# An attention and FFN sandwich on one core: probabilities and normalised x transposed through VectorE and DRAM in place of TensorE

## The chip, the cores and the metric

The kernel runs on one core of a Trainium2 chip. The metric is the device time of one execution in microseconds; the median of three runs of the kernel before is 426.01 us (425.57 to 428.9).

## The reference

For eight batches of 1024 rows of 256 numbers in float32:

```
x = x + layernorm(attn(layernorm(x)))        # one head, causal, Wq Wk Wv Wo of 256 x 256
x = x + layernorm(layernorm(x) @ W[idx] + b[idx])
attn(x): q = x@Wq; k = x@Wk; v = x@Wv
         softmax(mask(q k^T) / 16) v @ Wo
idx    = argmax(log_softmax(logits) - log(-log(u)))     # one of eight FFN weights
```

## The kernel before

A batch is cut into NT = 8 tiles of 128 rows, in NP = 4 pairs. Wq and Wk are folded into one matrix a, Wv and Wo into wvo, before the first batch. TensorE multiplies in a reduced float32 form; to keep precision each operand is kept as two halves: `hi` is rounded by ScalarE, `lo` is the value less `hi`, by VectorE. `product` (L805) makes three passes per block: lo x hi, hi x lo, hi x hi.

The steps of a batch, each named by a letter and a number in the order lists:

- S n: scores of row tile n against the n + 1 tiles up to it (two PSUM score buffers). M n (VectorE, L707): masks them, writes neg_scores, gives the row's maximum. E n (ScalarE, L549): exponentials to `probs`, with their sum.
- T n: TensorE transposes the n + 1 blocks of `probs` into one or two PSUM banks (L908); ScalarE rounds them to pT_hi (L441), VectorE subtracts to pT_lo (L613).
- V n: values of two tiles, with wvo. O n: probabilities times values, 3 (n + 1) products.
- O on ScalarE: sum of squares of the O row, and o_ez from the exponentials' sum; C n: variance on VectorE (o_ve, L735) and its power -1/2 on GpSimd (o_rstd, L387); R n (L741, VectorE): y = O x o_rstd + x, which frees the bank.
- N, K, Y, F, U, Z per pair: statistics of y (L749 to L756 on VectorE, power and shift on GpSimd), K: yn by ScalarE (L583), Y: its transposes (L932) and halves, F: product with the FFN weights, bias added by VectorE (L762), squares by ScalarE (L591), U: f_ve and f_rstd, Z (L778): out = f x f_rstd + y, then the store.
- L, H, X, G prepare the next batch: L statistics of x (L627 to L634 on VectorE, power and shift on GpSimd), H xn on ScalarE (L464), X transposes of xn per pair (L819) and halves, G n: a quarter of g = a^T xT, six products of 512 columns, and halves.

Each engine runs its own written list of steps (PE_ORDER, ACT_ORDER, DVE_ORDER, POOL_ORDER, and _LAST for batch 7). Batches 0 and 7 are straight-line code, batches 1 to 6 a hardware loop (Fori). All PSUM outputs except the scores rotate over four banks in the order of TensorE's list: a job waits until VectorE has drained the bank's previous one. The sync engine's queue issues four loads of x for the batch after next, each behind R of its pair, and then four stores.

Of the kernel before, what the change touches and what calls it, by code (L numbers as in the profile page):

```python
# [5 lines left out]
def sandwich_block_kernel(  # L6
# [28 lines left out]
    f32 = mybir.dt.float32  # L35
# [18 lines left out]
    PAR = NT * D  # L54

# [10 lines left out]
    PE_ORDER = """S0 V0 S1 V1 T0 S2 T1 S3 O0 V2 T2 O1 S4 T3 V3 O2 S5 O3 T4 S6 T5 S7 X0 Y0 O4 T6 O5 T7 O6 X1 Y1  # L66
        O7 F0 G0 Y2 X2 F1 X3 F2 Y3 G1 G2 F3 G3"""
    ACT_ORDER = """V0 E0 E1 V1 T0 E2 O0 T1 V2 T2 O1 E3 H0 T3 V3 E4 O2 O3 E5 T4 K0 T5 E6 K1 X0 Y0 O4 T6 E7 O5 T7
        H1 H2 O6 Y1 H3 X1 O7 K2 G0 Y2 F0 X2 K3 X3 F1 Y3 F2 G1 G2 F3 G3"""
    DVE_ORDER = """M0 M1 L0 V0 M2 T0 V1 L1 T1 C0 M3 R0 V2 L2 T2 M4 C1 V3 T3 R1 N0 M5 C2 C3 R2 R3 N1 M6 T4 T5 M7  # L70
        X0 Y0 C4 R4 T6 C5 L3 R5 T7 C6 N2 R6 X1 Y1 C7 F0 R7 N3 G0 Y2 F1 U0 X2 Z0 X3 F2 U1 Y3 U2 Z1 G1
        F3 Z2 U3 G2 G3 Z3"""
    POOL_ORDER = """C0 L0 L1 C1 C2 C3 N0 N1 C4 L2 C5 L3 C6 N2 C7 N3 U0 U1 U2 U3"""


    PE_LAST = """V0 S0 V1 S1 T0 S2 V2 T1 S3 O0 T2 O1 S4 T3 S5 O2 T4 O3 S6 V3 T5 O4 S7 Y0 T6 O5 T7 O6 Y1 F0 O7
        Y2 F1 F2 Y3 D11 Y4 F3 D12 F4"""
    ACT_LAST = """E0 V0 V1 T0 E1 V2 T1 E2 O0 E3 T2 O1 T3 E4 T4 O2 O3 E5 K0 E6 V3 T5 O4 Y0 T6 E7 O5 K1 T7 O6 Y1
        K2 F0 O7 Y2 K3 Y3 F1 K4 Y4 F2 F3 F4"""
    DVE_LAST = """M0 V0 M1 M2 V1 T0 V2 T1 C0 M3 M4 C1 R0 T2 R1 T3 N0 M5 C2 R2 C3 T4 M6 R3 V3 N1 C4 T5 R4 M7 Y0  # L80
        T6 C5 R5 T7 N2 C6 F0 R6 Y1 U0 N3 C7 Y2 F1 R7 N4 F2 Y3 U1 Z0 Z1 Y4 U2 F3 U3 F4 Z2 U4 Z3 Z4"""
    POOL_LAST = """C0 C1 C2 N0 C3 N1 C4 C5 N2 C6 U0 N3 C7 N4 U1 U2 U3 U4"""

    PE_BEFORE = "D22 W0 W1 D13 X0 A0 X1 D25 W2 G0 D6 X2 X3 G1 A1 G2 G3"
    ACT_BEFORE = "W0 H0 J0 H1 X0 A0 X1 B0 H2 H3 G0 J1 X2 X3 G1 U0 A1 U1 G2 U2 G3 E0"
    DVE_BEFORE = "L0 L1 W1 B0 J0 L2 L3 X0 A0 X1 W2 B1 G0 X2 X3 U0 G1 A1 U1 G2 G3"
# [3 lines left out]

    def tiles_of(unit, last):
# [17 lines left out]
    def jobs_of(steps):  # L112
        for kind, n in steps:
            if kind == "T":
                for g in range(len(t_groups(n))):
                    yield (kind, n, g)
            elif kind in "VOYFXGA":
                yield (kind, n, 0)

    SPLIT = "ATVYXG"
    def is_split(job):
        return job[0] in SPLIT

    def places(jobs, act_jobs, job0, split0):
        splits = {j: split0 + 1 + at for at, j in enumerate(filter(is_split, act_jobs))}
        return {j: (job0 + at, splits.get(j, 0)) for at, j in enumerate(jobs)}

    before = places(jobs_of(steps_of(PE_BEFORE)), jobs_of(steps_of(ACT_BEFORE)), 0, 0)  # L130
    JOB0, SPLIT0 = len(before), sum(map(is_split, before))
    full, final = (places(jobs_of(steps_of(pe)), jobs_of(steps_of(act)), JOB0, SPLIT0)
                   for pe, act in ((PE_ORDER, ACT_ORDER), (PE_LAST, ACT_LAST)))
    PER, SPER = len(full), sum(map(is_split, full))
    assert PER % NB == 0

    class Job:

        def __init__(self, b, last, kind, n, g=0, before=0):

            place, splits = (final if last else full)[(kind, n, g)]
            self.bank = place % NB
            self.offset = place // NB - before * (PER // NB)
            self.used = self.offset + b * (PER // NB)
            self.splits = splits + b * SPER

    class Before:
        def __init__(self, kind, n):  # L150
            place, self.splits = before[(kind, n, 0)]
            self.bank, self.offset = place % NB, place // NB
            self.used = self.offset

    def g_job(b, n):

        return Before("G", n) if isinstance(b, int) and b == 0 else Job(b, False, "G", n, before=1)

    x_rows = x.rearrange("b (t p) d -> b p t d", p=PART)
    out_rows = out.rearrange("b (t p) d -> b p t d", p=PART)  # L160

    ctx = ExitStack()
    with ctx:
# [41 lines left out]
        o_ez = sb("o_ez", [PART, NT])  # L205
        o_ve = sb("o_ve", [PART, NT])
# [26 lines left out]
        wf_raw = sb("wf_raw", [PART, KC, D])  # L233
# [4 lines left out]
        ident = sb("ident", [PART, PART])  # L238
        mask = sb("mask", [PART, S])
# [19 lines left out]
        hi_ready = sem("hi_ready")  # L259
        scores_ready = sem("scores_ready")  # L260
# [26 lines left out]
        halves_ready = sem("halves_ready")  # L287
        memsets = sem("memsets")
# [8 lines left out]
        wf_centred = sem("wf_centred")  # L297
        wf_hi_ready = sem("wf_hi_ready")
# [10 lines left out]

        def x_tile(b, t, n=1):  # L310

            return x_sb[:, bass.ds((b % 2) * PAR + t * D, n * D)]

        @block.sync
        def _(sp):
            def load_x(b, p, parity_at):
                sp.dma_start(x_sb[:, bass.ds(parity_at + 2 * p * D, 2 * D)],
                             x_rows[b, :, 2 * p:2 * p + 2, :]).then_inc(x_loaded[p], 16)

            def store(b, unit, last=False):  # L320
# [15 lines left out]
            load_x(0, 2, 0)  # L336
            load_x(0, 3, 0)
# [35 lines left out]
        def _(pool):  # L373
# [5 lines left out]
                                    pattern=[[-1, PART]], channel_multiplier=1).then_inc(consts_ready, 1)  # L379
            nc.gpsimd.memset(mask[:, :], 0.0).then_inc(memsets, 1)  # L380
# [38 lines left out]
            for p in range(NP):  # L419
                x_scales(0, p)  # L420
# [563 lines left out]
```

## Time and profile before

| | |
|---|---|
| median of three runs | 426.01 us |
| span of the profiled execution, from first to last instruction | 424.3 us (the page gives no other time of that execution) |
| busy: TensorE, VectorE, ScalarE, GpSimd | 98%, 80%, 71%, 28% |
| TensorE's own work on the chain that ended last | 93% |
| moved by DMA | 18.46 MB, 44 GB/s over the span |

Busy is the share of the span in which an engine executes something. Durations of single instructions overlap their successors on all engines, so what one costs in a row of many is read from the distance of starts. The chain that ended last is followed back from the last instruction and says which engine the time passed through.

### The profile page before, as it was taken

The page shows a single profiled execution, that of the slowest core. Times are in us where ns is not written, and L with a number is a line of the kernel's source. Part 1 is how long each engine was busy: PE and PEld are TensorE (multiplying, and loading weights), DVE is VectorE, ACT ScalarE, POOL GpSimd, SP SyncE. Part 2 cuts the span into 40 slices and gives each one's busy share as a digit, 9 for nine tenths or more (in the row PEclk, how much of TensorE's full clock was granted, in tenths as well). Part 3 has the DMA queues.
Part 4 walks back from the last instruction along what each step waited for, and adds up shares of the span by engine and source line. Part 5 has one row for each costly group of instructions (what it writes and reads, how often), then busy time and mean ns, then how long its engine had stood idle before and what let it go on. Part 6 is the DMA issues. An engine that isn't in the chain of part 4 may idle for free.

```text
span 424.3 us, 9812 instructions
## 1 busy us (share of the span) xinstructions
PE 414.0 (98%) x3045; PEld 393.2 (93%) x3045; DVE 339.8 (80%) x1010; ACT 299.1 (71%) x854; POOL 118.3 (28%) x237
## 2 busy tenths in 40 slices
PE   7999999999999999999999999999999999999993
PEld 7789999999999999999999999999999999999993
DVE  4578778987898878887788878898788887876776
ACT  5886877668766687568866687666885678756563
POOL 3103333232322232123421323223232224302133
PEclk9999999999999999999999999999999999999998
DMA  6310012110120101201021001201012000020003
GB/s 198 90 49 26 26 25 76 52 39 14 51 81 18 49 25 42 82 9 40 25 66 57 25 25 48 76 25 49 13 37 99 0 0 0 25 75 2 2 0 101
DMA packets 18951, 18.46 MB, mean 44 GB/s; under 512 B 1140, under 2 KB 18932, under 8 KB 18932
## 3 DMA queue, kind: packets, MB, share of 16 engines
q1 hardware_dynamic: 18660, 17.96, 13.5%
q10 hardware_dynamic: 272, 0.26, 0.2%
q8 instruction: 10, 0.16, 0.2%
q14 instruction: 9, 0.07, 0.1%
HBM read 9.83 MB, written 8.39 MB: 43 GB/s over the span
## 4 chain that ended last, share of the span: by engine, by line
PE 93%; DMA 2%; ACT 2%; DVE 1%; issue 0%; POOL 0%; SPq 0%; POOLq 0%; DVEq 0%
PE bank L805 54%; PE score L805 23%; PE bank L908 7%; PE bank L932 3%; PE bank L819 3%; DMA wq<-in_L_attn_Wq_dram 1%; DMA bias_raw<-in_L_ffn_b_dram 1%; PE score L891 1%; PE score L847 0%; PE bank L865 0%; POOL f_rstd L387 0%; PE score L835 0%; DVE out_sb L778 0%; ACT squares_junk L591 0%; ACT sums_junk L470 0%
## 5 line engine op out<-in xcount | busy, mean ns | idle before, releaser
L387 POOL TENSOR_TENSOR o_rstd<-o_ve,minus_half 128x1 f32<-128x1 f32 x64 | 35.2, 550 | 193.8 <-DVE o_ve L735 193.8
L805 PE MATMUL bank<-v_hi,pT_lo 128*128 128x256 f32 x288 | 84.6, 294 | 0.0
L805 PE MATMUL bank<-v_hi,pT_hi 128*128 128x256 f32 x288 | 81.4, 283 | 0.0
L805 PE MATMUL bank<-v_lo,pT_hi 128*128 128x256 f32 x288 | 81.3, 282 | 0.0
L805 PE MATMUL score<-xT_hi,g_lo 128*128 128x384 f32 (+4 forms) x176 | 63.7, 362 | 0.0
L805 PE MATMUL score<-xT_hi,g_hi 128*128 128x384 f32 (+4 forms) x176 | 61.1, 347 | 0.0
L805 PE MATMUL score<-xT_lo,g_hi 128*128 128x384 f32 (+4 forms) x176 | 61.1, 347 | 0.0
L549 ACT ACTIVATE probs<-neg_scores,neg_max 128x128 f32<-128x128 f32 (+3 forms) x64 | 49.7, 776 | 14.0 <-DVE neg_max L707 13.5
L805 PEld LDWEIGHTS bank<-v_lo,pT_hi 128*128 128x128 f32 x288 | 55.0, 191 | 0.4
L805 PEld LDWEIGHTS bank<-v_hi,pT_lo 128*128 128x128 f32 x288 | 54.9, 191 | 0.3
L805 PEld LDWEIGHTS bank<-v_hi,pT_hi 128*128 128x128 f32 x288 | 54.9, 191 | 0.0
L707 DVE CUSTOM_DVE_ANT_0 neg_scores<-score,mask 128x128 f32<-128x128 f32 (+3 forms) x64 | 48.2, 755 | 7.6 <-PE score L805 7.5
L574 ACT ACTIVATE squares_junk<-bank 128x256 bf16<-128x256 f32 x64 | 24.5, 383 | 40.3 <-PE bank L805 39.8
L613 DVE TENSOR_TENSOR pT_lo<-bank,pT_hi 128x384 fp32r<-128x384 f32 (+2 forms) x96 | 49.6, 551 | 0.8
L441 ACT ACTIVATE pT_hi<-bank 128x384 fp32r<-128x384 f32 (+2 forms) x96 | 43.1, 484 | 2.2 <-PE bank L908 2.0
L908 PE MATMUL bank<-ident,probs 128*128 128x128 f32 x288 | 42.0, 273 | 0.0
L741 DVE SCALAR_TENSOR_TENSOR y<-bank,o_rstd,x_sb 128x256 f32<-128x256 f32 x64 | 30.8, 481 | 11.1 <-POOL o_rstd L387 11.0
L591 ACT ACTIVATE squares_junk<-f_sb 128x256 bf16<-128x256 f32 x64 | 26.3, 419 | 16.7 <-DVE f_sb L762 16.7
L583 ACT ACTIVATE yn<-y,y_shift,y_rstd 128x256 f32<-128x256 f32 x64 | 35.0, 597 | 4.3 <-POOL y_shift L393 4.3
L387 POOL TENSOR_TENSOR f_rstd<-f_ve,minus_half 128x2 f32<-128x2 f32 (+1 forms) x33 | 24.1, 731 | 49.6 <-DVE f_ve L769 49.6
L805 PE MATMUL bank<-wf_hi,yT_lo 128*128 128x256 f32 x128 | 37.3, 292 | 0.4 <-DVE yT_lo L613 0.4
L805 PE MATMUL bank<-wvo_hi,xT_lo 128*128 128x256 f32 x128 | 36.9, 288 | 0.0
(112 smaller groups left out, 1130.5 us busy)
## 6 DMA issues: line engine op xcount, KB each, us to landing
x_sb<-in_L_attn_x_dram SPq DMA_DIRECT2D x32, 256.0 KB, 2.7
out_dram<-out_sb SPq DMA_DIRECT2D x31, 256.0 KB, 2.1
wq<-in_L_attn_Wq_dram ACTq DMA_DIRECT2D x1, 256.0 KB, 4.1
wk<-in_L_attn_Wk_dram SPq DMA_DIRECT2D x1, 256.0 KB, 4.4
wv<-in_L_attn_Wv_dram SPq DMA_DIRECT2D x1, 256.0 KB, 4.2
wo_raw<-in_L_attn_Wo_dram SPq DMA_DIRECT2D x1, 256.0 KB, 4.5
wf_raw<-in_L_ffn_W_dram SPq DMA_DIRECT2D x1, 256.0 KB, 2.7
out_dram<-out_sb SPq DMA_DIRECT2D x2, 128.0 KB, 2.1
```

What stands on the lines that cost most here:

```text
L387: return nc.gpsimd.tensor_tensor(dst[:, n0:n1], ve[:, n0:n1], minus_half[:, n0:n1], ALU.pow)
L441: nc.scalar.activation(dst, src, ACT.Identity).then_inc(hi_ready, 1)
L549: nc.scalar.activation(probs[:, n % 2, here], neg_scores[:, n % 2, here], ACT.Exp, scale=-1.0, bias=neg_max[:, n:n + 1], accum_out=exp_sum ...
L574: nc.scalar.activation(squares_junk[:, 0, n, :], cols(job.bank, D), ACT.Square, accum_out=o_ss[:, n:n + 1])
L583: last = nc.scalar.activation(yn[:, p, t % 2, :], y[:, t, :], ACT.Identity, bias=y_shift[:, t:t + 1], scale=y_rstd[:, t:t + 1])
L591: last = nc.scalar.activation(squares_junk[:, 1, t, :], f_sb[:, p, t % 2, :], ACT.Square, accum_out=f_ss[:, t:t + 1])
L613: nc.vector.tensor_tensor(dst, src, hi.bitcast(f32), ALU.subtract).then_inc(bank_drained[job.bank], 1)
L707: nc.vector.tensor_tensor_reduce(out=masked.rearrange("p (h w) -> p h w", h=h), in0=score[:, n % 2, 0:h, 0:w], in1=mask[:, here].rearrange ...
L741: nc.vector.scalar_tensor_tensor(out=y[:, n, :], in0=cols(job.bank, D), scalar=o_rstd[:, n:n + 1], in1=x_tile(b, n), op0=ALU.mult, op1=ALU ...
L805: last = nc.tensor.matmul(dst, l, r, start=(i == 0), stop=(i == len(passes) - 1))
L819: last = nc.tensor.transpose(cols(job.bank)[:, (2 * k + t) * PART:(2 * k + t + 1) * PART], xn[:, 2 * p + t, k * PART:(k + 1) * PART], iden ...
L908: last = nc.tensor.transpose(cols(job.bank)[:, (t - t0) * PART:(t - t0 + 1) * PART], probs[:, n % 2, t * PART:(t + 1) * PART], ident[:, :])
```

## The change

Probabilities (all of batches 0 to 6, tiles 0 to 3 of batch 7) and xn of batches 1 to 7 are no longer transposed by TensorE. VectorE transposes them in blocks of 32 x 32 (steps Q n and B p) into `p_turn` and `x_turn`; the sync queue writes each pair's buffer to DRAM (P p, and W for the whole of xn) and fetches it back in four DMAs, one for each 32 partitions, with the blocks exchanged between partitions (Q p, R 0). ScalarE rounds the `hi` halves from SBUF (P n, X n), GpSimd subtracts all `lo` halves of the probabilities and those of the second half of xT (X2, X3), VectorE those of the first half (X0, X1).

Other parts:

- y is transposed itself, without yn; F is scaled by y_rstd afterwards (two VectorE operations of 256 columns in place of one of 512). For this the FFN weights' column means are taken off at the start, by two products with a constant matrix.
- The exponentials' sum comes from O: v has two more columns (a constant and zero), so the O products have 258 columns; the squares of O and F take in a constant column, and o_ez, o_ve, f_ve, y_nm, y_ve, x_nm, x_ve leave ScalarE and VectorE. GpSimd adds eps and negates the mean itself.
- All batches are straight-line code; each list has steps of the batch before (marked '), and the sync queue has a list of its own. The new TensorE list puts all scores first. pT has three buffers in place of two; Z writes into f_sb and the store leaves from there.

```diff
-    PE_ORDER = """S0 V0 S1 V1 T0 S2 T1 S3 O0 V2 T2 O1 S4 T3 V3 O2 S5 O3 T4 S6 T5 S7 X0 Y0 O4 T6 O5 T7 O6 X1 Y1
-        O7 F0 G0 Y2 X2 F1 X3 F2 Y3 G1 G2 F3 G3"""
+    PE_ORDER = """S0 O6' Y2' S1 O7' S2 S3 V0 S4 S5 Y3' V1 S6 V2 S7 O0 O1 F1' V3 O2 F2' Y0 O3 F3' O4 O5 F0 G0 G1 Y1 G2 G3"""
+    ACT_ORDER = """G3' E0 O6' Y2' E1 H0 O7' H1 E2 H2 E3 V0 E4 P0 P1 Y3' E5 V1 H3 V2 E6 P2 O0 P3 O1 E7 F1' V3 O2 P4 P5 Y0 O3
+        F2' F3' O4 X0 X1 X2 O5 X3 F0 G0 P6 G1 P7 Y1 G2"""
+    DVE_ORDER = """Y1' G2' M0 G3' Q0 L0 L1 K0 M1 R6' Y2' Q1 K1 L2 B0 K2 M2 R7' B1 M3 Q2 N3' Q3 M4 V0 B2 M5 L3 Q4 Q5 K3 Y3'
+        V1 M6 B3 V2 Q6 M7 R0 F1' Q7 R1 V3 Z1' N0 R2 F2' Y0 F3' R3 N1 Z2' X0 X1 R4 F0 R5 Z3' N2 G0 Z0 G1"""
+    POOL_ORDER = """N2' C6' L0 L1 C7' L2 N3' P0 P1 L3 P2 C0 P3 C1 U1' C2 P4 P5 C3 U2' N0 C4 U3' N1 C5 X2 X3 U0 P6 P7"""
+    SP_ORDER = """P0 A3' Q0 P1 Q1 P2 W0 Q2 P3 R0 A0 Z1' Q3 A1 Z2' A2 Z3' Z0"""
+    PE_LAST = """V0 O6' S0 O7' S1 S2 S3 Y2' S4 S5 Y3' V1 V2 V3 O0 O1 S6 F1' Y0 O2 S7 O3 T4 T5 F2' F3' Y1 O4 T6 O5 F0 T7
+        O6 F1 Y2 O7 Y3 F2 F3 Y4 F4"""
...
+            def fetch(raw, kept, loaded):
+                for q, source in enumerate(kept):
+                    sp.dma_start(raw[q * QUAD:(q + 1) * QUAD].rearrange("a (i r) -> a i r", i=QUADS), source
+                                 ).then_inc(loaded, 16)
...
+                    elif kind == "W":
+                        sp.wait_ge(x_turned, b.count(NP, 0))
+                        sp.dma_start(x_kept.rearrange("p q r -> p (q r)"), x_turn[:, :]).then_inc(x_written, 16)
+                    elif kind == "R":
+                        sp.wait_ge(x_written, b.count(16, 0))
+                        fetch(x_turn[:, :], x_kept.rearrange("(i a) q r -> q a i r", i=QUADS), x_raw_loaded)
+                    elif kind == "P":
+                        sp.wait_ge(p_turned, b.count(NT, 2 * n + 2))
+                        sp.dma_start(p_kept[n].rearrange("p q r -> p (q r)"), p_slot(n)).then_inc(p_written[n], 16)
+                    elif kind == "Q":
+                        sp.wait_ge(p_written[n], b.count(16, 16))
+                        fetch(p_slot(n), p_kept[n].rearrange("(i a) q r -> q a i r", i=QUADS), p_loaded[n])
...  # GpSimd
+                    elif kind == "P":
+                        pool.wait_ge(p_hi_ready, b.count(NT, n + 1))
+                        nc.gpsimd.tensor_tensor(p_half(pT_lo, n), p_quads(n), p_half(pT_hi, n).bitcast(f32),
+                                                ALU.subtract).then_inc(p_lo_ready, 1)
...  # VectorE
+                    elif kind == "Q":
+                        dve.wait_ge(probs_ready, b.count(NT, n + 1))
...
+                        nc.vector.transpose(p_quads(n), probs[:, n % 2, 0:(n + 1) * PART].rearrange(
+                            "p (u q a) -> p u q a", q=QUADS, a=QUAD)).then_inc(p_turned, 1)
```

## Rows read from the trace of the kernel before

**Rows 1.** The page: span, busy times, TensorE in forty slices, chain by engine.

```profile
span 424.3 us, 9812 instructions
PE 414.0 (98%) x3045; PEld 393.2 (93%) x3045; DVE 339.8 (80%) x1010; ACT 299.1 (71%) x854; POOL 118.3 (28%) x237
...
PE   7999999999999999999999999999999999999993
...
PE 93%; DMA 2%; ACT 2%; DVE 1%; issue 0%; POOL 0%; SPq 0%; POOLq 0%; DVEq 0%
```

**Rows 2.** First products of a batch: all, then three starts in time order.

```profile
L891 PE MATMUL score<-xT_first,g_first x32: 271/275/377, 23.3 to 374.7; 128*128 128x128 f32 x32
...
223.20 0.61 PE L891 MATMUL score<-xT_first,g_first 128*128 128x128 f32 x4
273.11 0.61 PE L891 MATMUL score<-xT_first,g_first 128*128 128x128 f32 x4
...
374.36 0.61 PE L891 MATMUL score<-xT_first,g_first 128*128 128x128 f32 x4
```

**Rows 3.** TensorE in time order (start, us), and O6 in the chain.

```profile
203.03 1.06 PE L908 MATMUL bank<-ident,probs 128*128 128x128 f32 x8
203.84 0.36 PE L805 MATMUL bank<-v_hi,pT_lo 128*128 128x256 f32 x1
...
206.44 0.60 PE L819 MATMUL bank<-ident,xn 128*128 128x128 f32 x4
206.88 0.60 PE L932 MATMUL bank<-ident,yn 128*128 128x128 f32 x4
...
204.09 2.52 PE bank L805 x21
```

**Rows 4.** VectorE in time order: a stretch without waits, and two scale-and-adds.

```profile
229.15 0.29 DVE L613 TENSOR_TENSOR pT_lo<-bank,pT_hi 128x128 fp32r<-128x128 f32 x1
229.35 0.68 DVE L613 TENSOR_TENSOR v_lo<-bank,v_hi 128x512 fp32r<-128x512 f32 x1
229.95 0.74 DVE L627 BATCH_NORM_STATS2 x_stats<-x_sb 128x6 f32 x2
230.77 0.25 DVE L630 BATCH_NORM_AGGREGATE x_mv<-x_stats 128x2 f32<-128x6 f32 x2
231.05 0.17 DVE L633 TENSOR_SCALAR x_nm<-x_mv 128x2 f32<-128x2 f32 x1
...
224.97 0.87 DVE L778 SCALAR_TENSOR_TENSOR out_sb<-f_sb,f_rstd,y 128x256 f32<-128x256 f32 x2
225.76 0.28 DVE L707 CUSTOM_DVE_ANT_0 neg_scores<-score,mask 128x128 f32<-128x128 f32 x1
```

**Rows 5.** GpSimd in time order, then the exponentials (ns: shortest, median, longest).

```profile
1.61 0.95 POOL L380 MEMSET mask<- 128x1024 f32 x1
...
232.01 0.55 POOL L387 TENSOR_TENSOR o_rstd<-o_ve,minus_half 128x1 f32<-128x1 f32 x1 [7.41 <-DVE o_ve L735]
232.53 0.70 POOL L387 TENSOR_TENSOR x_rstd<-x_ve,minus_half 128x2 f32<-128x2 f32 x1
...
L549 ACT ACTIVATE probs<-neg_scores,neg_max x64: 390/775/1162, 27.0 to 400.9; 128x128 f32<-128x128 f32 x8, 128x256 f32<-128x256 f32 x8, 128x384 f32<-128x384 f32 x8, 128x512 f32<-128x512 f32 x8
```

**Rows 6.** Stretches (last: clock, DMA share, GB/s); an issue; KB and us to landing.

```profile
4.00:6.00 2.00, 1.35 (x8) 1.05 (x6) 1.24 (x6) 0.00 (x0) 0.01 (x1) 1.00 1.09 371
20.00:25.00 5.00, 4.36 (x26) 3.52 (x25) 1.75 (x4) 4.41 (x13) 0.00 (x0) 1.00 0.54 187
...
0.75 0.45 SPq L317 DMA_DIRECT2D x_sb<-in_L_attn_x_dram  x1
...
x_sb<-in_L_attn_x_dram SPq DMA_DIRECT2D x32, 256.0 KB, 2.7
out_dram<-out_sb SPq DMA_DIRECT2D x31, 256.0 KB, 2.1
```

More of the change, by code:

```diff
@@ L110, in pieces, with __init__, count, other @@
         return (1, w) if w <= BANK else (2, w // 2)
-    def jobs_of(steps):
-        for kind, n in steps:
+    class Batch:
+        def __init__(self, s, ahead):
+            self.known = s + ahead
+            self.first, self.last = self.known == 0, self.known == B - 1
+        def count(self, per, extra):
+            return self.known * per + extra
+        def other(self, by):
+            return Batch(self.known, by)
+        def exists(self, first=0):
+            return first <= self.known < B
@@ L114, in jobs_of @@
+    def jobs_of(turns):
+        for kind, n, ahead in turns:
             if kind == "T":
                 for g in range(len(t_groups(n))):
[L116 to L134, printed above, removed]
+                    yield (kind, n, g, ahead)
+            elif kind in "VOYFG":
+                yield (kind, n, 0, ahead)
+    PE_TURNS, PE_LAST_TURNS = turns_of(PE_ORDER), turns_of(PE_LAST)
@@ L149, in sandwich_block_kernel @@
     class Before:
         def __init__(self, kind, n):
[L151 to L157, printed above, removed]
+            place = BEFORE_JOBS.index((kind, n))
+            self.bank, self.used = place % NB, place // NB
+            self.offset = self.used
+            self.splits = BEFORE_SPLITS.index((kind, n)) + 1
@@ L159, in sandwich_block_kernel, with places_of, follows @@
+    def places_of(order, last):
+        at = {}
+        for s in range(B):
+            for kind, n, ahead in turns_of(order if s < B - 1 else last):
+                at[(kind, n, s + ahead)] = len(at)
+        return at
+    in_dve, in_act = places_of(DVE_ORDER, DVE_LAST), places_of(ACT_ORDER, ACT_LAST)
+    def follows(places, then, first):
+        return first in places and places[first] < places[then]
     x_rows = x.rearrange("b (t p) d -> b p t d", p=PART)
     out_rows = out.rearrange("b (t p) d -> b p t d", p=PART)
+    x_kept = nc.dram_tensor("x_kept", (PART, QUADS, RUN), f32, kind="Internal").ap()
@@ L162, in sandwich_block_kernel @@
+    p_kept = [nc.dram_tensor(f"p_kept{p}", (PART, QUADS, (4 * p + 3) * QUAD), f32, kind="Internal").ap()
+              for p in range(NP)]
     ctx = ExitStack()
@@ L308, in cols, with raw_block, split_block, p_slot @@
             return bank[bk][:, 0:n]
+        def raw_block(c, k):
+            cols_of = x_turn[:, :].rearrange("p (i k t s) -> p k t i s", i=QUADS, k=KC, t=NT)
+            return cols_of[:, k, c * (NT // 2):(c + 1) * (NT // 2), :, :]
+        def split_block(half, c, k):
+            return half[:, k, c * BANK:(c + 1) * BANK].rearrange("p (t i s) -> p t i s", t=NT // 2, i=QUADS)
+        def p_slot(p):
+            at = sum(4 * q + 3 for q in range(p)) * PART
+            return p_turn[:, at:at + (4 * p + 3) * PART]
@@ L369, in _ @@
+            sequence(0, SP_ORDER)
+            for s in range(1, B - 2):
+                sequence(s, SP_ORDER)
+            sequence(B - 2, SP_ORDER)
+            sequence(B - 1, SP_LAST)
             for p in range(NP):
@@ L404, in sequence @@
+            def sequence(s, text):
+                for kind, n, ahead in turns_of(text):
+                    b = Batch(s, ahead)
+                    if not b.exists(kind in "LX"):
+                        continue
+                    t0, t1, p = tiles_of(n, b.last)
                     if kind == "L":
-                        x_scales(b + 1, n)
+                        x_scales(b, n)
                     elif kind == "C":
-                        pool.wait_ge(o_ve_ready, b * NT + n + 1)
-                        rstd(o_rstd, o_ve, n, n + 1).then_inc(o_rstd_ready, 1)
+                        pool.wait_ge(o_squares, b.count(NT, n + 1))
+                        rstd(o_rstd, o_ss, n, n + 1).then_inc(o_rstd_ready, 1)
@@ L426, in _ @@
+            for p in range(NP):
+                x_scales(Batch(0, 0), p)
+            sequence(0, POOL_ORDER)
+            for s in range(1, B - 1):
+                sequence(s, POOL_ORDER)
+            sequence(B - 1, POOL_LAST)
         @block.scalar
@@ L593, in sequence @@
                         last.then_inc(f_squares, 1)
[L595 to L598 removed]
+            sequence(0, ACT_ORDER)
+            for s in range(1, B - 1):
+                sequence(s, ACT_ORDER)
+            sequence(B - 1, ACT_LAST)
         @block.vector
@@ new lines, in sequence @@
+                        for t in range(t0, t1):
+                            last = nc.vector.scalar_tensor_tensor(out=f_sb[:, p, t % 2, 0:D],
+                                                                  in0=bank[job.bank][:, (t - t0) * D:(t - t0 + 1) * D],
+                                                                  scalar=y_rstd[:, t:t + 1], in1=bias[:, :],
+                                                                  op0=ALU.mult, op1=ALU.add)
+                        last.then_inc(bank_drained[job.bank], 1)
```

630 lines of the change are left out of this document (376 added, 254 removed).

## The prediction

> **What bounds the kernel now.** I read the page first: busy shares, the forty slices and the chain of waits [rows 1]. TensorE is busy 98% of a span of 424.3 us, in every slice but the ends, and 93% of the chain that ended last is its own work. VectorE is at 80%, ScalarE at 71%, GpSimd at 28%. The first products of a batch (S0) then give the period [rows 2]: 273.11 - 223.20 = 49.91 us. The first S0 is at 23.3, the last at 374.36, so the span is 23.3 of preparation, 351.1 for seven batches, and 49.9 for the last. TensorE waits for practically nothing inside a period, so taking work off it pays one for one until another engine or a transfer sets the pace.
>
> **What leaves TensorE.** From the start of a group to the next start, eight transposes of probabilities take 203.84 - 203.03 = 0.81, and the product behind them starts its successor 0.08 later than usual, so 0.89 or 0.11 each; a group of four of xn takes 206.88 - 206.44 = 0.44, 0.11 each [rows 3]. A batch has 36 of probabilities and 16 of xn for the next batch: 52 x 0.11 = 5.7 us. The products are untouched: O6's 21 take 2.52, 0.12 each [rows 3], and two more columns on 256 for the 108 O products add 108 x 0.12 x 2/256 = 0.1. TensorE's own need per batch is then 49.9 - 5.7 + 0.1 = 44.3 us. In the last batch only 10 of the 36 leave (1.1 us). The work that the new order carries into the next batch (O6', O7', Y2', Y3', F1' to F3') is 45 + 36 products and 8 transposes, 81 x 0.12 + 0.9 = 10.6 us: it leaves batch 0 and arrives in the last.
>
> **VectorE.** Its real price is the distance of starts, not the duration [rows 4]: 128 columns take 229.35 - 229.15 = 0.20, 512 take 229.95 - 229.35 = 0.60, so a width w costs 0.07 + 1.04 ns x w; two scale-and-adds take 225.76 - 224.97 = 0.79, 0.40 each; two bn_stats with their drain 0.82, two bn_aggr 0.28, and the two small operations behind them end 0.15 later. Per batch of now: M 5.4, pT_lo 5.6, four groups of four 512-wide low halves 9.6, statistics 8 x 1.26 = 10.1, R, Z 3.2 each, F 2.4, o_ve and f_ve 1.3: 40.8, which is the 80%. Removed: pT_lo 5.6, half of xT_lo 1.2, x_nm, x_ve, y_nm, y_ve, o_ve, f_ve 8 x 0.15 + 1.3 = 2.5. Added: F as eight scale-and-adds +0.8, and the 32x32 block transposes, which no row shows. They write as many columns as M reads: 8 x 0.07 + 4608 x 1.04 ns = 5.4 for the probabilities (Q) and 8 x (0.07 + 0.27) = 2.7 for xn (B). That takes one column per 1.04 ns, the nearest row of the same engine and type; at half that rate they would be 7 us dearer, at twice it 3.5 cheaper. Sum: 40.8 - 9.3 + 0.8 + 8.1 = 40.4 us of 44.3, 91%. So VectorE may idle 3.9 us per batch where it now idles 9. I went through the order by hand with these prices: before S7 it has 21.2 us of work in 22.8 of TensorE's, and every M is done before the S two further on asks for it.
>
> **ScalarE** loses yn (64 x 0.6 now), o_ez and the accumulator reads of the exponentials, and P replaces the rounding of pT_hi at equal width. It is lighter and not on the path, except E7, 1.16 us [rows 5], which stands behind P3 and O1.
>
> **GpSimd** gets P (4608 columns) and half of X (1024). It has shown only a memset, 0.95 us for 1024 columns, and powers of one and two columns, 0.55 and 0.70 [rows 5]. The memset's 0.93 ns a column is the low end. [...] What is queued behind P matters more: C3 (o_rstd) stands behind P4 and P5, but O3's bank is wanted only four jobs later, 5.4 us on.
>
> [...]
>
> **Transfers.** Each probability and xn goes to DRAM and back: 2.36 MB and 1.05 MB per batch each way, 6.8 MB beside today's 2.1. Two rates stand in the trace: 371 GB/s while eight loads are queued, 187 in a stretch with the engines half idle [rows 6]; I take the first, as these transfers queue up too, and keep the second for the range. An issue takes the queue 0.45 us, a 256 KB load lands after 2.7, a store after 2.1 [rows 6]; less 0.7 of moving, 1.4 to 2.0 fixed. Four fetches are 1.9 us of issue; 33 issues per batch are 15 us.
>
> The chain that decides, from the end of S7 (t = 0): O1 ends 1.1, ScalarE's square 1.8, E7 3.0, block transpose Q7 (1.1) 4.8 behind F1'. The sync queue holds R0 (xn's return) behind P3 (the last pair's write), which waits for Q7. P3: issue 5.3, 960 KB 2.6, landed 9.4. R0: 1 MB more, landed at 5.3 + 2.6 + 2.8 + 2.0 = 12.7. X0 and X1 on ScalarE and then VectorE: 15.7. TensorE wants G0 after O0 to F0, 123 products and a group of four: 14.8 + 0.4 = 15.2, a stall of 0.5. [...]
>
> **The sum.** Period 44.3 + 0.5 for G0 + 1.0 for VectorE's dependences (an estimate: a quarter of the 3.9 it may idle) = 45.8. Batch 0 has 33.7 of TensorE's work but nothing to lay over the chain: 2.0 for VectorE before S7, and 15.7 - (15.2 - 4.3) = 4.8 at G0, so 40.5. Last batch 49.9 - 1.1 + 10.6 + 1.0 for waits = 60.4. The FFN's column means are two products at the start, and the loop's end costs nothing now. 23.3 + 40.5 + 6 x 45.8 + 60.4 = 399.0. The page gives no time but the span; the median 426.0 is 1.7 above it, so 400.7, and I say **400 us**, 6% faster.
>
> **Rivals.**
> 1. VectorE becomes the bound. Against the forecast: 91% load, and stops of 0.3 to 0.8 us for ScalarE and GpSimd all through its timeline now. If it keeps idling the 9.1 us of today, the period is 40.4 + 9.1 = 49.5, or its operations stretch that much beside a GpSimd that is no longer idle, the total is 23.3 + 42 + 297 + 60.4 + 1.7 = 424; if half of the excess comes, 47.6 and 413. For the forecast: many of those stops are now waits for TensorE itself. 0.2, taken at 413.
>
> The trace shows GpSimd 28% busy with one or two columns, so nothing of how it and VectorE disturb each other. [...]
>
> 2. Transfers at 187 GB/s. R0 lands at 5.3 + 5.1 + 5.6 + 2.0 = 18.0, G0 waits until 21, 5.8 late: period 50.1, total 23.3 + 45.8 + 300.6 + 61 + 1.7 = 432; midway 416. For it: 8.9 MB per batch at 371 GB/s already take 24 of 46 us. Against: the 187 was a stretch limited by issue. 0.1, half of it within 1%.
> 3. **Slower.** The fetches write 32 partitions each in runs of 384 to 2048 bytes, a shape no row has. Below 187 GB/s the wait for xn at G0 eats more than the 5.7 us saved; at 140 R0 lands at 21.7, G0 is 9.5 late, the period 53.8, the total 23.3 + 49.5 + 322.8 + 61 + 1.7 = 458. 0.07.
> 4. No stall beyond batch 0: period 44.3, total 23.3 + 39 + 265.8 + 60.4 + 1.7 = 390. 0.13.
>
> The forecast itself (393 to 408) gets 0.5. About 1% is what a measurement tells from no change. Faster by over 1%: 0.5 + 0.13 + most of rival 1 and a part of 2 = 0.83; within 1%: 0.08; slower: 0.09. The range reaches from a little below rival 4 to the dear side of rival 1: 388 to 419.
>
> **What would show it.** Right: S0 to S0 at 45 to 46.5 us, TensorE busy 96% or more, no transposes of probabilities but the last batch's, x_raw landing 12 to 13 us after S7. Rival 1: VectorE over 93% busy, TensorE waiting for max or drained banks, Z over 0.5 us. Rivals 2 and 3: TensorE waits at G0 for xT_lo, GpSimd and ScalarE's X idle on the DMA. [...] The prediction fails if block transposes take twice a column's time or the chain after S7 is more than 3 us longer than I laid it out.

## The result, and the profile after

The changed kernel takes 440.97 us (median of six runs, 436.71 to 444.4) against 426.26 for the kernel before (median of six, 425.57 to 428.9): 1.033 times as long, 95% interval 1.030 to 1.035, a ratio that leaves out the slow one of the six runs, 444.4. The forecast was 400, with 388 to 419 as its range. The profiled execution has a span of 434.9 us and took 436.71, 1.8 above its span; it is the fastest of the six, so the sums below explain the lower edge of what was measured.

The page of the changed kernel: busy times, forty slices, the chain by engine and line, and the groups that answer to [rows 4] and [rows 5] (busy us, mean ns, idle before and its releaser).

```profile
span 434.9 us, 7841 instructions
PE 390.4 (90%) x2652; PEld 362.5 (83%) x2652; DVE 343.5 (79%) x830; ACT 259.5 (60%) x642; POOL 231.8 (53%) x381
PE   7979779999789987999799997999879998799994
...
PEclk9999899999889999999889998999889999999998
DMA  5414891379714797159923799059932598121022
...
PE 51%; DVE 15%; DMA 13%; issue 7%; SPq 4%; ACT 4%; POOL 3%; POOLq 2%; DVEq 0%
...
L544 POOL TENSOR_TENSOR pT_lo<-p_turn,pT_hi 128x128 fp32r<-128x128 f32 (+7 forms) x60 | 84.2, 1420 | 55.8 <-ACT pT_hi L710 55.7
...
L985 DVE SCALAR_TENSOR_TENSOR f_sb<-f_sb,f_rstd,y 128x256 f32<-128x256 f32 x64 | 51.8, 849 | 2.7 <-POOL f_rstd L501 2.6
...
x_turn<-x_kept SPq DMA_DIRECT2D x28, 256.0 KB, 7.1
p_kept<-p_turn SPq DMA_DIRECT2D x7, 960.0 KB, 5.1
p_turn<-p_kept SPq DMA_DIRECT2D x28, 240.0 KB, 8.5
```

TensorE did lose work (busy 390.4 us), but unlike in [rows 1] it has a gap in every batch: slices of 7 or 8 recur in every batch, at or right behind the slices in which the DMA row stands at 9, and in five of the seven batches the clock row dips to 8 there too. Z (`L985`), whose pair took 0.79 in [rows 4], now averages 0.85 us an instruction.

The waits of the changed kernel (us in total, times, longest) name two late inputs:

```profile
ACT xT_first L734 <- DMA x_turn<-x_kept: 21.0, 7, 3.8
...
PE bank L1009 <- DVE xT_lo L937: 16.4, 7, 3.1
...
ACT pT_hi L710 <- DMA p_turn<-p_kept: 15.1, 12, 3.1
...
PE score L1117 <- DVE g_lo L773: 7.7, 4, 2.5
```

Seven times G0 waits for xT_lo (1.7 us in batch 0, 14.7 in the six others), and behind that ScalarE waits for the returned xn. Four times S0 waits for g_lo. The chain of waits through one period shows the first (start, us, what):

```profile
246.48 2.50 PE bank L1009 x21
...
249.94 1.16 DVE p_turn L917
...
251.12 0.34 SPq L464
...
251.50 0.43 SPq L441
...
253.87 7.90 DMA x_turn<-x_kept
...
261.79 0.51 ACT xT_first L734 x2
...
262.85 0.55 DVE xT_lo L937
...
263.46 0.70 DVE xT_lo L937
...
264.20 4.61 PE bank L1009 x12
```

S7 ends at 246.48, which is t = 0 of the forecast's chain. Q7 ends at 4.6 (forecast 4.8), P3 is issued at 4.6 (forecast 5.3), and then the row of 7.90: xn's return lands at 15.3, not 12.7. G0 starts at 17.7, 2.5 later than TensorE was to want it. Its first twelve products take 4.61 us; at 0.23 each, the distance of their starts at full clock around 366 us, they take 2.8.

The stretches of the changed kernel while the last write of probabilities is issued, around G0, and at the end of the next period (busy time and count of TensorE, its weight loads, VectorE, ScalarE and GpSimd, then granted clock, DMA share, GB/s) show what the engines and the clock did:

```profile
250.00:254.00 4.00, 3.95 (x34) 3.75 (x33) 3.96 (x10) 2.49 (x8) 1.53 (x2) 1.00 1.08 290
...
262.00:264.00 2.00, 0.00 (x0) 0.00 (x0) 1.15 (x2) 2.00 (x6) 0.00 (x0) 1.00 1.14 275
264.00:266.00 2.00, 1.80 (x5) 1.46 (x6) 2.00 (x6) 1.38 (x6) 1.71 (x2) 0.69 1.06 210
266.00:268.00 2.00, 2.00 (x6) 1.58 (x5) 2.00 (x3) 1.03 (x4) 2.00 (x3) 0.50 1.08 249
268.00:270.00 2.00, 2.00 (x11) 1.60 (x11) 1.97 (x7) 1.19 (x3) 0.53 (x2) 0.96 0.89 304
...
320.00:322.00 2.00, 0.48 (x3) 0.06 (x1) 2.00 (x1) 0.61 (x2) 2.00 (x1) 1.00 0.00 0
322.00:324.00 2.00, 0.98 (x5) 0.98 (x5) 2.00 (x4) 0.00 (x0) 1.11 (x3) 0.70 0.33 118
```

The DMA engines are wholly taken at 210 to 290 GB/s, where [rows 6] had 371. TensorE stood idle for 2.3 us before 264.2 and then works at half clock (granted 0.50). The second loss is in 320 to 322: no transfer runs, TensorE is idle for most of it, and VectorE and GpSimd are each in one instruction. Time order in the changed kernel, GpSimd first, then VectorE, then the S0 that waited:

```profile
313.42 2.71 POOL L550 TENSOR_TENSOR xT_lo<-x_turn,xT_hi 128x512 fp32r<-128x512 f32 x2
...
317.45 4.63 POOL L544 TENSOR_TENSOR pT_lo<-p_turn,pT_hi 128x896 fp32r<-128x896 f32 x2 [0.48 <-ACT pT_hi L710]
...
313.84 0.47 DVE L954 SCALAR_TENSOR_TENSOR y<-bank,o_rstd,x_sb 128x256 f32<-128x256 f32 x1
314.24 2.17 DVE L985 SCALAR_TENSOR_TENSOR f_sb<-f_sb,f_rstd,y 128x256 f32<-128x256 f32 x2
...
317.85 4.52 DVE L985 SCALAR_TENSOR_TENSOR f_sb<-f_sb,f_rstd,y 128x256 f32<-128x256 f32 x2
322.29 0.68 DVE L773 TENSOR_TENSOR g_lo<-bank,g_hi 128x512 fp32r<-128x512 f32 x1
...
323.02 1.22 PE L1117 MATMUL score<-xT_first,g_first 128*128 128x128 f32 x4 [2.54 <-DVE g_lo L773]
```

Two Z take 4.52 us (2.02 and 2.58) while GpSimd's two subtractions, of 896 and then of 1024 columns (the row prints the first one's shape), take 4.63. Each Z ends 0.29 us after the subtraction beside which it started, at 319.87 behind 319.58 and at 322.37 behind 322.08. This holds all through the trace: 21 Z start while such a subtraction runs, and each ends 0.28 to 0.29 us after it; four start less than 0.4 us ahead of one and take their usual 0.47 to 0.49. So a Z is not slowed by a factor: it lasts for what is left of GpSimd's instruction and 0.3 us more. R, which reads PSUM, took 0.47 at 313.84 beside the same GpSimd row that held the Z behind it. The g_lo that S0 needs stands behind the two Z, S0 comes 2.54 late, and its own four products run at half clock.

The two losses make up whole periods. From S0 at 223.15 to S0 at 271.85 it is 48.7 us: 44.6 of need (shown below), 2.3 waiting at G0, 1.8 for g at half clock. From there to 323.02 it is 51.2: 44.6, 2.15 waiting at G0, 2.54 at S0, and 1.6 for g at half clock (its first twelve products take 4.33 us, from 312.80 to 317.13); 0.3 is left over.

### The profile page after: what moved, and what is told of

It is laid out like the page before. It is cut to its first block, busy times and chain, and to the rows that moved or that the text cites. A ratio compares the mean times of both kernels' runs of the same rounds, so it can differ in the third digit from the quotient of the medians.

```text
span 434.9 us, 7841 instructions
## 1 busy us (share of the span) xinstructions
PE 390.4 (90%) x2652; PEld 362.5 (83%) x2652; DVE 343.5 (79%) x830; ACT 259.5 (60%) x642; POOL 231.8 (53%) x381
## 2 busy tenths in 40 slices
DMA packets 45611, 67.75 MB, mean 156 GB/s; under 512 B 8196, under 2 KB 38276, under 8 KB 44676
## 4 chain that ended last, share of the span: by engine, by line
PE 51%; DVE 15%; DMA 13%; issue 7%; SPq 4%; ACT 4%; POOL 3%; POOLq 2%; DVEq 0%
PE bank L1009 28%; PE score L1009 20%; DMA x_turn<-x_kept 13%; DVE f_sb L985 6%; SPq L441 4%; DVE p_turn L917 2%; PE bank L1163 2%; DVE f_sb L976 2%; DVE g_lo L773 1%; PE score L1117 1%; DVE xT_lo L937 1%; ACT xT_hi L736 1%; POOLq L515 1%; ACT probs L701 1%; DVE y L954 1%
## 5 line engine op out<-in xcount | busy, mean ns | idle before, releaser
L544 POOL TENSOR_TENSOR pT_lo<-p_turn,pT_hi 128x128 fp32r<-128x128 f32 (+7 forms) x60 | 84.2, 1420 | 55.8 <-ACT pT_hi L710 55.7
L1009 PE MATMUL bank<-v_hi,pT_lo 128*128 128x258 f32 x288 | 84.9, 295 | 2.4 <-POOL pT_lo L544 1.4
L1009 PE MATMUL bank<-v_lo,pT_hi 128*128 128x258 f32 x288 | 82.6, 287 | 0.0
L1009 PE MATMUL bank<-v_hi,pT_hi 128*128 128x258 f32 x288 | 82.3, 286 | 0.0
L501 POOL TENSOR_TENSOR o_rstd<-o_ss,minus_half 128x1 f32<-128x1 f32 x64 | 36.9, 576 | 51.9 <-ACT squares_junk L744 51.8
L985 DVE SCALAR_TENSOR_TENSOR f_sb<-f_sb,f_rstd,y 128x256 f32<-128x256 f32 x64 | 51.8, 849 | 2.7 <-POOL f_rstd L501 2.6
L608 ACT ACTIVATE xn<-x_sb,x_shift,x_rstd 128x256 f32<-128x256 f32 x64 | 34.9, 593 | 27.1 <-POOL x_shift L516 25.0
L710 ACT ACTIVATE pT_hi<-p_turn 128x128 fp32r<-128x128 f32 (+7 forms) x60 | 38.2, 662 | 15.3 <-DMA p_turn<-p_kept 15.1
L917 DVE STREAM_TRANSPOSE p_turn<-probs 128x128 f32<-128x128 f32 (+7 forms) x60 | 44.2, 746 | 3.6 <-ACT probs L701 3.1
L744 ACT ACTIVATE squares_junk<-bank 128x257 bf16<-128x257 f32 x64 | 24.5, 382 | 37.9 <-PE bank L1009 37.1
L1009 PE MATMUL bank<-xT_hi,a_lo 128*128 128x512 f32 x64 | 30.4, 475 | 16.7 <-DVE xT_lo L937 16.4
```

Source lines behind the costliest of these rows:

```text
L501: return nc.gpsimd.tensor_tensor(dst[:, n0:n1], ve[:, n0:n1], minus_half[:, n0:n1], ALU.pow)
L544: nc.gpsimd.tensor_tensor(p_half(pT_lo, n), p_quads(n), p_half(pT_hi, n).bitcast(f32), ALU.subtract).then_inc(p_lo_ready, 1)
L608: last = nc.scalar.activation(xn[:, t, :], x_tile(b, t), ACT.Identity, bias=x_shift[:, t:t + 1], scale=x_rstd[:, t:t + 1])
L710: nc.scalar.activation(p_half(pT_hi, n), p_quads(n), ACT.Identity).then_inc(p_hi_ready, 1)
L744: nc.scalar.activation(squares_junk[:, 0, n, 0:D + 1], cols(job.bank, D + 1), ACT.Square, scale=D ** -0.5, accum_out=o_ss[:, n:n + 1]).the ...
L917: nc.vector.transpose(p_quads(n), probs[:, n % 2, 0:(n + 1) * PART].rearrange("p (u q a) -> p u q a", q=QUADS, a=QUAD)).then_inc(p_turned, 1)
```

## The experiments

All ran in three rounds beside the kernel before, whose medians there were 425.7 to 426.0. The theory: the period is set by two waits, xn's late return at G0 and Z held by GpSimd's subtractions ahead of g_lo. The rival for each experiment is in its expectation.

**e1, xn fetched ahead of the last write of probabilities.**

```
- SP_ORDER = """... Q2 P3 R0 A0 ..."""
+ SP_ORDER = """... Q2 R0 P3 A0 ..."""
```

> The sync queue fetches xn back (R0) before it waits for the last pair of probabilities (P3). In the trace of the changed kernel xn is in DRAM at about 250 us of the period from 223, R0 is issued at 251.5 behind P3 and lands at 261.8, G0 starts 2.5 us late and TensorE then runs at half its clock for two quarters of g. If the transfer chain is the main cause, R0 lands about 3 us earlier, G0 waits for nothing, and with the clock kept the period falls from 51 to 46-47: about 410 us. If VectorE's operations with two SBUF inputs behind GpSimd are the main cause, Z stays at up to 2.5 us, S0 stays late for g_lo and the total falls by 10 us at most, to 430 or more. A third possibility is that the last pair comes back too late now, as P3 is issued some 2 us later: then O6 waits for pT_lo.

Measured 422.66 us (420.2 to 425.26), 0.992 of before (0.988 to 0.996). The waits of that kernel:

```profile
ACT pT_hi L710 <- DMA p_turn<-p_kept: 36.9, 14, 4.4
...
PE bank L1009 <- POOL xT_lo L550: 6.4, 6, 1.3
PE score L1117 <- DVE g_lo L773: 6.3, 5, 2.3
```

18 us come back by two entries in SyncE's order: the wait at G0 falls from 16.4 to 6.4. That is not the earlier xn alone. The probabilities return later now, so GpSimd's last subtractions miss some of the Z: the 64 Z take 39.3 us in all, where the changed kernel has 51.8. The edit eases both waits and doesn't price either by itself. And the write of 960 KB behind it now lands after 9.3 us instead of 5.1, and ScalarE waits for probabilities (36.9, was 15.1): the queue's delay moved to the other return.

**e2, Z moved away from GpSimd's subtractions.** Z3' stands ahead of R4, Z0 behind M1 of the next batch (its store on SyncE with it).

```
- DVE_ORDER = """Y1' G2' M0 G3' Q0 L0 L1 K0 M1 R6' ... X0 X1 R4 F0 R5 Z3' N2 G0 Z0 G1"""
+ DVE_ORDER = """Y1' G2' M0 G3' Q0 L0 L1 K0 M1 Z0' R6' ... X0 X1 Z3' R4 F0 R5 N2 G0 G1"""
```

> The Z steps that lie beside GpSimd's long subtractions are moved: Z3' directly behind X1, Z0 into the next batch behind M1, where GpSimd has only operations of one and two columns; the store goes with it. If VectorE is held up by GpSimd while both have two SBUF inputs, Z falls from a mean of 849 ns to below 600 and the wait of S0 for g_lo (about 2.5 us in three of seven periods, and half clock behind it) goes: 425 to 430 us. If the length of Z had another cause, it moves with it. G0 still waits for xn, so a period does not fall below 48.

Measured 420.97 us (419.8 to 421.29), 0.987 (0.984 to 0.990). F and Z in the changed kernel, R in the same, and then Z in this one (durations in ns: shortest, median, longest; first and last start):

```profile
L976 DVE SCALAR_TENSOR_TENSOR f_sb<-bank,y_rstd,bias x64: 472/476/485, 62.5 to 430.2; 128x256 f32<-128x256 f32 x64
...
L985 DVE SCALAR_TENSOR_TENSOR f_sb<-f_sb,f_rstd,y x64: 450/480/2579, 66.1 to 431.9; 128x256 f32<-128x256 f32 x64
```

```profile
L954 DVE SCALAR_TENSOR_TENSOR y<-bank,o_rstd,x_sb x64: 440/478/486, 46.9 to 426.7; 128x256 f32<-128x256 f32 x64
```

```profile
L985 DVE SCALAR_TENSOR_TENSOR f_sb<-f_sb,f_rstd,y x64: 451/479/489, 73.6 to 416.1; 128x256 f32<-128x256 f32 x64
```

The hold is gone with the same work on every engine: 20 us, more than the 11 to 16 expected. R and F read a PSUM bank and one SBUF tensor, and none of their 128 instructions exceeded 0.49 us even in the changed kernel, though 45 of them lay for more than half of their length beside one of GpSimd's subtractions; Z reads two SBUF tensors and went to 2.58. That it is the second SBUF input that counts is inferred from this contrast: no run changed the inputs of Z, and VectorE's other operation with two, xT_lo, never ran beside such a subtraction. The 20 us also hold what it is worth to have Z's ordinary 0.85 us a pair out of the way of g_lo, which no run separates. The wait at G0 stays (15.5 us, 7 times).

**e3, both.** The edits of e1 and e2 together.

> Both edits: xn fetched before the last pair is written, and Z moved away from GpSimd's long subtractions. If these two waits with the clock that each costs are the whole loss, the period is 45 to 46.5 and the total 400 to 408 us, below both kernels. If the transfers themselves are too slow (engines fully taken at 210 to 275 GB/s), TensorE still waits in each batch for xn or for the last pair and the total stays over 415.

Measured 422.86 us (422.09 to 423.8), 0.993 (0.990 to 0.995). The gains do not add, and the total is in the range expected if the transfers themselves are too slow. TensorE still waits for g_lo (10.0 us, 6 times), though Z no longer delays it: ScalarE stands in P6 waiting for probabilities (32.5 us) with G1's g_hi queued behind. So with Z moved, the order of the returns decides who waits, and hardly how much.

**e4, xn's return cut to a quarter.** The changed kernel with xn's fetches reading one of four runs per partition; three quarters of xn's returned blocks are left out.

```
- fetch(x_turn[:, :], x_kept.rearrange("(i a) q r -> q a i r", i=QUADS), x_raw_loaded)
+ fetch(x_turn[:, :], x_kept.rearrange("(i a) q r -> q a i r", i=QUADS), x_raw_loaded, 1)
```

> Leaves out three quarters of xn's return: each of the four fetches brings one of its four runs, so 0.25 MB in place of 1 MB, in the same number of issues; the rest of x_turn keeps what VectorE wrote. Order unchanged. If the bytes of the return set the wait at G0, it lands about 2.5 us earlier and the wait and the half clock behind it go: 8 to 20 us off. If the issue of four DMAs (2.8 us) and the fixed time set it, less than 1 us of landing goes, and the total stays over 435.

Measured 435.85 us (432.43 to 437.79), 1.024 (1.021 to 1.027): 5 us off, where 8 to 20 were expected. Each fetch of xn lands after 4.0 us instead of 7.1, and the wait of G0 for VectorE's xT_lo goes (5.5 us on GpSimd's xT_lo and 3.0 on g_lo are left), but S0 waits 14.8 us for g_lo instead of 7.7, and the 64 Z take 57.7 us, up from 51.8. By itself the earlier xn is worth 5 us: Z's hold lies next on the path and takes the rest.

**e5, the whole preparation of xn earlier.** e2, with L3, K3, H3 and B3 moved forward, R0 ahead of P3, X0 and X1 ahead of F3', and ScalarE's P6 behind G1.

```
- ... E5 V1 H3 V2 E6 P2 O0 ... F2' F3' O4 X0 X1 X2 O5 X3 F0 G0 P6 G1 P7 Y1 G2      (ScalarE)
+ ... H3 E5 V1 V2 E6 P2 O0 ... F2' X0 X1 F3' O4 X2 O5 X3 F0 G0 G1 P6 P7 Y1 G2
```

> On top of Z moved away from GpSimd: xn's way is spread. The last pair of xn is prepared some 3 us earlier in the batch (L3, K3, H3, B3), xn comes back before the last pair of probabilities is written, X0 and X1 are done earlier, and ScalarE rounds P6 only after G1, since with xn fetched first it stood waiting for P6's data with g's second quarter behind it. If the order of the transfers is what costs, G0 and S0 wait for nothing any more: period 45.5 to 46.5, total 402 to 409 us. If the transfer engines' capacity is what costs (they are fully taken at about 250 GB/s for 15 us of each batch), some other step waits in their place and the total stays at 415 or more.

Measured 420.2 us (417.21 to 421.32), 0.988 (0.985 to 0.990): the best version that computes everything, level with e2, and 1.2% better than the kernel before, but not the 402 to 409 that the order alone would have given. The chain and the stretches of it:

```profile
242.61 7.84 DMA p_kept<-p_turn
...
252.49 5.29 DMA p_turn<-p_kept
...
257.80 0.96 ACT pT_hi L710
...
258.83 2.14 POOL pT_lo L544
```

```profile
240.00:244.00 4.00, 2.82 (x22) 2.42 (x21) 3.96 (x10) 3.50 (x9) 2.88 (x4) 1.00 1.10 223
244.00:248.00 4.00, 4.00 (x36) 4.00 (x36) 3.00 (x9) 2.76 (x9) 3.77 (x3) 1.00 1.08 235
248.00:252.00 4.00, 4.00 (x35) 4.00 (x34) 3.90 (x11) 3.26 (x12) 2.56 (x5) 1.00 0.93 330
252.00:256.00 4.00, 4.00 (x24) 3.22 (x23) 2.88 (x8) 1.51 (x6) 3.86 (x6) 1.00 1.05 228
```

With xn out of the way the chain runs through the probabilities: 7.8 us to write, 5.3 to fetch, in sixteen microseconds in which the DMA engines' share never falls under 0.93.

**e6, the clock held up at G0.** 40 small products of no effect on the output are put ahead of G0 in the changed kernel, started once the last row maximum is ready.

```
+ pe.wait_ge(max_ready, b.count(NT, NT)); keep_warm(40)      (ahead of G0)
```

> The changed kernel with 40 small products on no one's data ahead of G0, in the time in which TensorE waits for xn (2.2 to 3.3 us per batch; they take about 2.4 us at full clock). Nothing else moves. If the granted clock falls because of that wait and the first two quarters of g then pay double, they run in 2.8 us in place of 4.6, and 7 x 1.5 = 10 us go, unless S0 waits the longer for g_lo behind Z, which the edit does not touch: 431 to 439 us. If the clock falls for another reason, the total does not fall, or rises by up to 1 us per batch.

Measured 441.09 us (437.99 to 443.12), 1.035 (1.029 to 1.041), as the changed kernel, and not the 431 to 439 expected. The granted clock is now 1.00 in every stretch from 266.5 to 275 us, where g is computed, and G0 waits only 2.1 us in all; but S0 waits 12.3 us for g_lo, six times (was 7.7, four). At G0 the clock fell to 0.50 in four of seven batches of the changed kernel and falls in none here: the half clock at G0 came from the wait and went with it, but what that gave was lost again at S0, behind Z, as the expectation allowed.

**e7, every return cut to a quarter, on e2.** Of all turned blocks three quarters are not fetched.

```
- ....rearrange("a (i r) -> a i r", i=QUADS), source
+ ....rearrange("a (i r) -> a i r", i=QUADS)[:, 0:1], source[:, 0:1]
```

> Leaves out three quarters of every fetch from DRAM (one of four runs each, of xn and of the probabilities), with Z moved away from GpSimd; writes, issues and order are unchanged. The total is what the order gives with nearly free returns. If transfers are what keeps the kernel with Z moved (421 us) from the 400 forecast, it comes to 398 to 408. If it stays above 412, the rest is not bandwidth but issue time, fixed latency and the steps of the other engines.

Measured 392.52 us (392.38 to 393.26), 0.922 (0.920 to 0.925), below the 398 to 408 expected. One period of it, in the columns of the stretches above:

```profile
242.10:286.70 44.60, 44.55 (x316) 42.30 (x315) 38.95 (x103) 30.68 (x77) 30.19 (x47) 1.00 0.43 144
```

TensorE is busy all the time at full clock, and a period is 44.6 us; VectorE, with 39.0 us busy, leaves it waiting for 0.05.

**e8, all of xT_lo on VectorE.** The changed kernel with X2 and X3 behind X1 on VectorE, none on GpSimd.

> Undoes one part of the change: all four low halves of xT on VectorE, none on GpSimd. VectorE gets 2 x 0.6 us per batch more behind X1, GpSimd 2.7 us less, so P6 and P7 start earlier and Z3' no longer lies beside X2 and X3. If sharing with GpSimd is what VectorE pays, Z gets shorter by about as much as X costs, and the total stays within 1.5% of the changed kernel, 435 to 447 us; if GpSimd's part was a gain, it is slower by 8 us or more.

Measured 443.43 us (441.75 to 444.14), 1.040 (1.037 to 1.043). By the medians the split between VectorE and GpSimd is worth 2.5 us, though single runs overlap, and it is not what fails; Z still goes to 2.58 us beside pT_lo.

**e9, every return cut to a quarter, Z left in place.** The fourth corner of the square of returns (full or a quarter) and Z (in place or moved).

> The changed kernel, Z where the change has it, with every fetch of turned blocks cut to one of its four runs per partition (three quarters of the returned bytes are left out, so most of xT and pT is computed from old data). It is the fourth corner of a square: returns full or short, Z beside GpSimd or moved. The other three stand at 440.97 us (full, beside), 420.97 (full, moved) and 392.52 (short, moved). Theory 1, the hold of Z by GpSimd is a cost of its own: g_lo comes late for S0 in every period by the 2 to 3 us that the waits on g_lo showed with the full returns (2.5 to 2.9 us each), so 7 x 2.8 = 20 us on 392.5, near 412; Z still has instructions of 2.3 us or more. Rival, Z was held only because the late returns pushed GpSimd's subtractions of P6 and of xT against it: with short returns those end earlier, Z stays under 0.7 us, and the time is 393 to 396.

Measured 424.4 us (423.22 to 429.77), 0.995 (0.992 to 0.998). Z and the waits of that kernel:

```profile
L985 DVE SCALAR_TENSOR_TENSOR f_sb<-f_sb,f_rstd,y x64: 451/483/2572, 61.3 to 420.2; 128x256 f32<-128x256 f32 x64
```

```profile
PE score L1117 <- DVE g_lo L773: 15.1, 6, 2.9
```

| us | Z beside GpSimd | Z moved | Z's hold costs |
|---|---|---|---|
| returns full | 440.97 | 420.97 | 20.0 |
| returns a quarter | 424.4 | 392.52 | 31.9 |
| volume of the returns costs | 16.6 | 28.5 | |

The rival (Z is held only because late data pushes GpSimd against it) falls. The hold costs more by itself than beside the late returns, 31.9 where 20 was expected. TensorE's waits for g_lo are 15.1 + 3.0 of it, and the other 13.8 are TensorE's own slower work: it is busy for 388.1 us where e7 has 374.3, with the same 2652 instructions, and its granted clock is 0.969 in the mean against 0.995. Alone, the returns cost 28.5 and the hold 31.9; together they cost 48.5, so 11.9 of it are common to both.

## Why the prediction was wrong

**Held: what leaves TensorE.** The need per period was forecast at 44.3; e7 shows 44.6. The whole of e7 splits into 22.7 to the first S0, 41.2 for batch 0, five periods of 44.6, and 104.0 for the last two (forecast, with one stall term of 1.0 still in it, 44.3 + 60.4). Rival 4 (no stall, 390) is about what the kernel does once the returns are small and Z is out of GpSimd's way. That batch 0's 41.2 lies near the forecast's 40.5 is luck: the forecast had 33.7 of TensorE's work, 2.0 for VectorE and 4.8 of stall at G0, while e7 shows TensorE busy for 35.9 us, no wait at G0, and 5.3 of idle time elsewhere, most of it in waits for VectorE's maxima (2.8) and for y (2.3).

**Held: the block transposes, VectorE's load, the chain up to P3.** Q7 took 1.16 (forecast 1.1). All 60 transposes of probabilities are 44.2 us of durations; their starts lie 0.07 closer each (Q7: 1.23 long, 1.16 to the next), which makes 40.0, and the forecast was 7 x 5.4 + 1.6 = 39.4. VectorE was no bound in e7.

**Failed, first step: transfers at 371 GB/s.** "As these transfers queue up too" was the reason for taking the upper rate, and it is the step that failed: with writes and fetches of short runs mixed, engines that are wholly taken move 210 to 290 GB/s. R0's landing at 12.7 in the chain became 15.3, and "a stall of 0.5" at G0 became 2.3 in the period shown. TensorE waited there 16.4 us in seven batches, where 6 x 0.5 + 4.8 = 7.8 was forecast; batch 0 had 1.7 of it instead of 4.8, and the six others 2.45 each. From the issue of P3 to the landing of R0 it took 10.65 us (251.12 to 261.77) for 2.03 MB; less the forecast's 2.0 fixed that is 235 GB/s, and the forecast had 7.4. That is rival 2's mechanism at a rate nearer to its 187 than to 371; rival 2's midway would have given 416. Its price left out a second effect, the one I did not list at all: after the idle stretch, g's products ran at a granted clock of 0.50, 1.8 us more in one period and 1.6 in the next. Over the whole execution TensorE is busy for 16.1 us more than in e7 (390.4 against 374.3, the same 2652 instructions, mean clock 0.965 against 0.995), so its slower work, most of it the lower clock (an estimate: 0.035 x 434.9 - 0.005 x 390.7 = 13.3 us), is over a third of the 44.2 us by which the two spans differ. The sign that the forecast gave for its own failure, the chain after S7 over 3 us longer, did not show: xT_lo of VectorE was done at 17.7 instead of 15.7.

**Failed, second step: Z at 0.40.** The forecast left Z's distance unchanged, and rival 1 let VectorE's operations stretch beside GpSimd to a period of 47.6, 413 in total. Z went to five times its length (2.58 us against 0.48), ending 0.28 to 0.29 us behind GpSimd's instruction, 21 times of 21, and e2 prices that at 20 us, e9 and e7 at 32. The trace of before had no long GpSimd instruction beside a Z, so nothing in it could price this; rival 1's size for it, half of an excess, was my estimate and had no row behind it. Z has two SBUF inputs; R and F, with one and a PSUM bank, never went over 0.49 us.

**Mis-sized: GpSimd.** I reckoned with 1.9 ns a column, an estimate at twice the memset's 0.93 [rows 5]; 84.2 us for the 33,536 columns of pT_lo are 2.5, and the 18.9 us for the 7,168 of xT_lo are 2.6. It matters through Z, since each Z that started beside a subtraction lasted to its end.

**The balance of the profiled execution.** Forecast span 399.0, measured 434.9:

| stretch | forecast | after | e7 |
|---|---|---|---|
| to the first S0 | 23.3 | 22.2 | 22.7 |
| batch 0 | 40.5 | 47.3 | 41.2 |
| five periods | 229.0 | 253.5 | 222.8 |
| last period and batch | 106.2 | 111.9 | 104.0 |

Batch 0 is 6.8 over and e7 gives back 6.1 of it. The five periods are 24.5 over and e7 gives back 30.7: there, the period is 50.7 against the forecast's 45.8. The sign of the error came from taking the two losses as rivals, with 0.2 and 0.1: they are different places of one period, they both happened, and together they cost 6.1 us in each of the five periods (50.7 - 44.6) against a saving of 5.3; in all, by the medians, 440.97 - 392.52 = 48.5 us. The result is slower, as rival 3 had it at 0.07, but not by rival 3's mechanism: G0 waited 2.45 us on average and not 9.5.

**Open.** Why the mixed transfers move only 210 to 290 GB/s was not tested by itself: a quarter of the fetched bytes comes with a quarter of the packets (31,403 in all in e7, 45,611 in the changed kernel), so e7 does not tell volume from the number of short runs. No version that keeps the probabilities' turn through DRAM and leaves xn on TensorE was tried.

## What to carry to other kernels

When work leaves the bounding engine, lay the whole chain of one period out with the slower of the rates that the trace shows, and look for long GpSimd instructions beside those of VectorE whose duration the trace shows only without one; Z, with two SBUF inputs, lasted to the end of the subtraction that it started beside, 21 times of 21, up to 2.58 us where it took 0.48 alone. Move such a step before trusting its duration: e2 moved Z, and it kept to 0.49. Two losses that you have listed as rivals can both happen; their prices then do not add, as what one gives back the next one takes (e3, e4, e6), so an experiment on one alone under- or overstates it, and only the square (e2, e7, e9) sizes both. An order written by hand is worth several trials: here 18 to 20 us came from moving one or two entries, and turned 3% slower into about 1% faster.

## What the runs showed of the hardware

- VectorE's scale-and-add with two SBUF inputs, 0.48 us alone, took up to 2.58 us when it started beside one of GpSimd's subtractions of 512 to 1024 columns (1.3 to 2.6 us each), and ended 0.28 to 0.29 us after it, 21 times of 21; started just ahead of one, it kept its 0.48, four times of four. With one input in PSUM it stayed below 0.49 in 128 instructions, 45 of them beside a subtraction.
- GpSimd's two-input subtraction: 2.5 to 2.6 ns a column of 128 partitions in the mean of all.
- A 32x32 block transpose of 1024 fp32 columns on VectorE: 1.16 us, as a subtraction of that width would take by [rows 4].
- DRAM round trips with fetches of 32 partitions in four runs each: DMA share 1.05 to 1.14 at 210 to 290 GB/s (330 in one stretch of e5, at 0.93), and 256 KB land after 7.1 us where loads in [rows 6] took 2.7.
- TensorE's granted clock fell to 0.50 for 3.4 us (once 6.8) at six of the changed kernel's eight pauses of 2.1 to 3.1 us, and stayed at 1.00 at the other two (2.16 us before 365.45, 2.95 before 375.28) and at the three of 1.6 to 2.0; it also fell at 49.7, where the pause was 1.34. With small products ahead of G0 (e6) it fell at none of the seven G0, and at four in the changed kernel.
